# A two-round graph network kernel: 80 raw tiles per round instead of 64, the first 32 one per half iteration, and the raw bias added in place in PSUM

## The reference, cut to what matters

```python
h = relu(bn(x, gamma, beta))                 # batch norm over all nodes
h = einsum('nd,od->no', h, w) + b            # w is (T*D, D): 640 outputs per node
msg = h.reshape(N, T, D)[src, etype]         # one 128-wide row per edge
x = segment_sum(msg, dst, N)
```

## Time and profile before

| what | value |
|---|---|
| median of 3 runs | 6475.83 us |
| profiled execution | 6482.43 us |
| its span | 6480.6 us, mean granted TensorE clock 0.727 of 2.4 GHz |
| first round's gathers start | 164.42 us |
| raw gathers of round 2 start | 2074.29 us |
| second round's gathers start | 2181.80 us |

### The profile page before, as it was taken

One profiled execution on the slowest core, in us unless ns is written; L12 is line 12 of the kernel. 1 busy time (PEld: TensorE's weight loads), 2 busy tenths in 40 slices (PEclk: granted clock), 3 DMA queues, 4 the chain that ended last, 5 costly groups with the idle time before them and its releaser, 6 DMA issues. The chain is left out here.

```text
span 6480.6 us, 66649 instructions
## 1 busy us (share of the span) xinstructions
PE 4158.0 (64%) x17271; PEld 2806.2 (43%) x17271; DVE 3822.2 (59%) x7438; ACT 1611.9 (25%) x3872; POOL 4619.0 (71%) x4787
## 2 busy tenths in 40 slices
PE   7445454544445645455454555778777889999898
PEld 4333343433334434334343444333323346666696
DVE  6544444443334777776676666544444457777698
ACT  4000000000001200000000000576666656666504
POOL 5777777777777677777777777577777777777604
PEclk9555555555556755655555676898898889999999
DMA  9211121212223521221222333333333356777696
GB/s 342 53 52 52 52 53 52 52 52 55 65 65 117 188 52 52 53 52 52 52 52 53 86 90 92 99 117 110 110 110 110 110 174 217 220 219 216 208 315 211
DMA packets 432604, 726.45 MB, mean 112 GB/s; under 512 B 104654, under 2 KB 206576, under 8 KB 431506
## 3 DMA queue, kind: packets, MB, share of 16 engines
q1 hardware_dynamic: 281652, 400.74, 19.7%
q0 software_dynamic: 150592, 321.58, 17.0%
HBM read 509.16 MB, written 212.75 MB: 111 GB/s over the span
## 5 line engine op out<-in xcount | busy, mean ns | idle before, releaser
L573 POOL DMA_INDIRECT edge_rows<-messages,idx_stage x1504 | 1446.1, 961 | 487.1 <-issue 457.9
L1658 PE MATMUL banks<-onehot,edge_rows 128*128 128x128 f32 x3008 | 715.9, 413 | 995.7 <-DMA edge_rows<-messages,idx_stage 960.8
L1658 PEld LDWEIGHTS banks<-onehot,edge_rows 128*128 128x128 f32 x3008 | 613.8, 303 | 1117.2 <-DMA edge_rows<-messages,idx_stage 1082.0
L630 POOL DMA_INDIRECT sorted_rows<-edge_rows,idx_stage x784 | 760.3, 970 | 276.3 <-issue 238.2
L630 POOL DMA_INDIRECT sorted_rows<-buf_a,idx_stage x784 | 760.5, 970 | 260.5 <-issue 241.4
L573 POOL DMA_INDIRECT buf_x<-messages,idx_stage x747 | 717.4, 960 | 227.7 <-issue 227.7
L573 POOL DMA_INDIRECT buf_a<-messages,idx_stage x747 | 714.5, 957 | 227.7 <-issue 227.7
L1040 DVE TENSOR_TENSOR buf_a<-buf_a,banks 128x128 f32 x375 | 108.1, 288 | 1044.3 <-PE banks L1658 1005.4
L689 ACT ACTIVATE h_stage<-banks,bn_shift,bn_scale 128x128 f32<-128x128 f32 x128 | 58.6, 458 | 2521.1 <-PE banks L1599 2521.1
L1658 PE MATMUL banks<-x_onehot,buf_x 128*128 128x128 f32 x1494 | 355.9, 413 | 490.6 <-DMA buf_x<-messages,idx_stage 490.5
L1658 PE MATMUL banks<-x_onehot,buf_a 128*128 128x128 f32 x1494 | 344.8, 403 | 459.9 <-DMA buf_a<-messages,idx_stage 459.5
(11 more groups left out here) (201 smaller groups left out, 7088.3 us busy)
## 6 DMA issues: line engine op xcount, KB each, us to landing
buf_a<-sorted_rows SPq DMA_DIRECT2D x593, 288.0 KB, 4.0
messages<-work SPq DMA_DIRECT2D x196, 320.0 KB
buf_a<-dst_rows SPq DMA_DIRECT2D x198, 256.0 KB
buf_a<-in_attr SPq DMA_DIRECT2D x198, 128.0 KB, 2.5
buf_a<-h_in SPq DMA_DIRECT2D x396, 64.0 KB
edge_rows<-messages,idx_stage POOLq DMA_INDIRECT x1504, 2.5
sorted_rows<-edge_rows,idx_stage POOLq DMA_INDIRECT x784
sorted_rows<-buf_a,idx_stage POOLq DMA_INDIRECT x784
```

The lines of the kernel that those rows point to most:

```text
L573: nc.gpsimd.indirect_dma_start(gathered[p][h][:, t, :], None, source, bass.IndirectOffsetOnAxis(ap=idx_stage[:, h, t:t + 1], axis=0),).the ...
L630: nc.gpsimd.indirect_dma_start(sorted_rows, bass.IndirectOffsetOnAxis(ap=idx_stage[:, 2 * u + h, t:t + 1], axis=0), msg_halves[2 * u + h][ ...
L1658: last = nc.tensor.matmul(ps_sums[p][slot][j], rows_in_slot[:, j * GROUP_TILES + t, :], hot[:, j * GROUP_TILES + t, :], start=(t == 0), st ...
```

## The change

The number of raw tiles per round goes from 64 to 80 (`RAW_ITERS` from 4 to 5). The first 32 of them (`RAW_TWICE`) are processed one per half, the others one per two halves. Turn and transform of a tile now lie in the same half on TensorE, the turn before the second group and the transform behind it; bias, product and type sum are in VectorE's next half. The bias sum writes back into PSUM, the product reads it there, and `turn_raw` waits for the product. The masks and the types move to other free places, in two parts. The memsets of the accumulators are cut in two; in round 1 the first part runs ahead of the raw gathers, in round 2 likewise, after a wait for raw sums of round 1. The conv buffers `f_sb` and `msg_halves` move in `buf_a`; the row of ones in `f_sb` is written after round 2 instead of before it, and the first attribute loads follow the first `y` chunk. The slot of a half is now its number modulo 4, the first half of a round being half 10.

```diff
-RAW_ITERS = (4, 4)
+RAW_ITERS = (5, 5)
+RAW_TWICE = 2 * 16
-MSG_COLS = 16 * 512
+MSG_COLS = 20 * 512
...
+        def raw_tile(p, k):
+            n = k - 2 * RAW_ITERS[p]
+            if n >= RAW_TWICE:
+                n = RAW_TWICE + (n - RAW_TWICE) // 2 if n % 2 == 0 else -1
+            return n if 0 <= n < RAW_ITERS[p] * ITER_TILES else None
+        def raw_half(p, k):
+            t = raw_tile(p, k)
+            return t // HALF_TILES if t is not None and t % HALF_TILES == HALF_TILES - 1 else None
...
             load_x(0)
+            sp.wait_ge(s_y, 1)
+            load_x(1)
             for h in range(2):
                 load_attributes(h, h)
-            sp.wait_ge(s_y, 1)
-            load_x(1)
...
+            nc.gpsimd.memset(buf_a[:, 0:6 * WIDE], 0.0).then_inc(s_clear[0], 1)
             pool.wait_ge(s_edges_in, 64)
             pool.wait_ge(s_node_out, 16 * CHUNKS)
             gather_raw(0)
-            nc.gpsimd.memset(buf_a[:, :], 0.0).then_inc(s_clear[0], 1)
+            nc.gpsimd.memset(buf_a[:, 6 * WIDE:NBUF], 0.0).then_inc(s_clear[0], 1)
             for rnd in range(2):
                 if rnd == 1:
+                    pool.wait_ge(s_raw_agg, 2 * RAW_ITERS[0])
+                    pool.wait_ge(s_acc[0], SUMS + 2)
+                    nc.gpsimd.memset(buf_x[:, 0:RAW_TILES * P], 0.0).then_inc(s_clear[1], 1)
                     pool.wait_ge(s_node_out, 16 * CHUNKS * 2)
                     gather_raw(1)
                     pool.wait_ge(s_closed, 2)
-                    nc.gpsimd.memset(buf_x[:, :], 0.0).then_inc(s_clear[1], 1)
+                    nc.gpsimd.memset(buf_x[:, RAW_TILES * P:NBUF], 0.0).then_inc(s_clear[1], 1)
...
                 for t in range(T):
-                    link(nc.vector.tensor_scalar(raw_mask[:, :, t], raw_type, float(t), None, ALU.is_equal))
+                    for masks, types in zip(raw_masks, (raw_type[:, 0:masks_apart], raw_type[:, masks_apart:RAW_TILES])):
+                        link(nc.vector.tensor_scalar(masks[:, :, t], types, float(t), None, ALU.is_equal))
...
+        raw_biased = ps_raw.rearrange("p (t d) -> p t d", t=T)
...
-                nc.vector.tensor_tensor(raw_biased, ps_raw.rearrange("p (t d) -> p t d", t=T),
+                nc.vector.tensor_tensor(raw_biased, raw_biased,
                                         b_types[p][:, :].rearrange("p (t d) -> p t d", t=T), ALU.add).then_inc(s_raw_biased, 1)
...
-                nc.vector.tensor_tensor(raw_picked, raw_biased, raw_mask[:, t, :].unsqueeze(2).broadcast_to([P, T, D]),
+                mask = raw_masks[t >= masks_apart][:, t % masks_apart, :]
+                nc.vector.tensor_tensor(raw_picked, raw_biased, mask.unsqueeze(2).broadcast_to([P, T, D]),
...  round_half
+                t = None if beyond else raw_tile(p, k - 1)
-                    t = r - RAW_ITERS[p] - 1
-                    if h == 0 and 0 <= t < raw:
+                    if t is not None:
                         bias_raw(p, t)
...
-                    if h == 0 and 0 <= t < raw:
+                    if t is not None:
                         pick_raw(p, t)
...
-                    if h == 0 and 0 <= t < raw:
+                    if t is not None:
                         message_raw(p, t)
...  after the second round
+            nc.vector.memset(f_sb[RBF:RBF + 1, :, :, :], 1.0).then_inc(s_cut, 1)
...  turn_raw
-                    pe.wait_ge(s_raw_biased, n)
+                    pe.wait_ge(s_raw_picked, n)
...  aggregate
-                    if j and not beyond and 0 <= r - RAW_ITERS[p] < raw:
-                        (turn_raw, transform_raw)[h](p, r - RAW_ITERS[p])
+                    if j and raw is not None:
+                        turn_raw(p, raw)
...
+                    if raw is not None:
+                        transform_raw(p, raw)
```

More of the change, by code:

```diff
@@ L94 @@
 assert ITERS % 2 == 0 and FIRST_ITERS % 2 == 0 and CHUNK_ITERS % 2 == 0
-assert all(n % 2 == 0 and (2 * HALF_TILES // 2 + 1) * n + HALF_TILES + 2 <= CHUNK_ITERS + RAW_TILES for n in RAW_ITERS)
+assert all(2 * n + 2 * n * ITER_TILES - RAW_TWICE + 4 <= 2 * CHUNK_ITERS for n in RAW_ITERS)
 assert X_COLS * X_PARTS == N and X_COLS % BN_CHUNK == 0 and GROUPS % 4 == 0
@@ L215, in gnn_program @@
         x_in, squares, centred = (work[:, i * WIDE:(i + 1) * WIDE] for i in range(3))
-        square_sum, sd, rstd = (buf_a[:, 10432 + 8 * i:10436 + 8 * i] for i in range(3))
+        square_sum, sd, rstd = (buf_a[:, NPAD + 8 * i:NPAD + 4 + 8 * i] for i in range(3))
         h_rows = buf_a[:, 8 * WIDE:9 * WIDE]
@@ L566, in gather_pass @@
                     pool.wait_ge(s, v)
[L567 to L576, removed]
+                for half in range(2 * RAW_ITERS[p], 2 * ITERS):
+                    h = half % GATHER_SLOTS
+                    pool.wait_ge(s_idx[p], half + (1 - 2 * RAW_ITERS[p]))
+                    for t in range(LAST_TILES if half == 2 * ITERS - 1 else HALF_TILES):
+                        nc.gpsimd.indirect_dma_start(
+                            gathered[p][h][:, t, :], None, source,
+                            bass.IndirectOffsetOnAxis(ap=idx_stage[:, h, t:t + 1], axis=0),
+                        ).then_inc(s_gather[h][t // GROUP_TILES], 16)
             def gather_raw(p):
@@ L1225, in round_loop @@
                 whole = end // 2 - (end == ITERS)
-                for r2 in turns(dve, first // 2, whole, beyond):
+                for r in range(first, first + first % 2):
+                    bases = load_bases(r)
+                    for h in range(2):
+                        round_half(p, acc, r, r % 2, h, i, bases, beyond)
+                for r2 in turns(dve, (first + 1) // 2, whole, beyond):
                     for u in range(2):
@@ L1237, in hots_ahead @@
             def hots_ahead(p):
-                for half in range(1, AHEAD):
-                    build_onehot(p, 2 * RAW_ITERS[p] + half, half)
+                for half in range(2 * RAW_ITERS[p], 2 * RAW_ITERS[p] + AHEAD):
+                    build_onehot(p, half, half % GATHER_SLOTS)
             def count_beyond():
+                build_onehot(0, 2 * RAW_ITERS[0], 0)
                 raw_beyond(0, buf_a)
@@ L1637, in aggregate @@
                 r = r2 * 2 + u
-                turn, raw = r2 - RAW_ITERS[p] // 2, RAW_ITERS[p] * ITER_TILES
+                raw = None if beyond else raw_tile(p, r * 2 + h)
                 closing = isinstance(r2, int) and r2 == PAIRS - 1 and 2 * u + h == GATHER_SLOTS - 1
@@ L1663, in aggregate @@
                 else:
[L1664 to L1666 removed]
+                    if raw is not None:
+                        transform_raw(p, raw)
+                    if raw_half(p, r * 2 + h - 2) is not None:
+                        sum_raw(p, raw_half(p, r * 2 + h - 2))
             def mean(m):
@@ L1687, in round_loop @@
                 whole = end // 2 - (end == ITERS)
-                for r2 in turns(pe, first // 2, whole, beyond):
+                for r in range(first, first + first % 2):
+                    for h in range(2):
+                        aggregate(p, r // 2, r % 2, h, beyond)
+                for r2 in turns(pe, (first + 1) // 2, whole, beyond):
                     for u in range(2):
```

52 lines of the change are left out of this document (25 added, 27 removed).

## The result

The changed kernel takes 6464.02 us (median of 22 runs, 6458.64 to 6467.6) against 6474.41 for the kernel before beside it (22 runs, 6468.95 to 6478.03): ratio 0.9984, 95% interval 0.9977 to 0.9990, 10.4 us less. The forecast was +1.6.

What follows compares the result with a forecast made beforehand. POOL's gathers bound the rounds. -20.3 + 4.9 + 1.5 - 20.2 + 35.1 + 0.6 = +1.6 us, 6477.4 against the median 6475.83; range 6463 to 6491, with the faster cases 6440 to 6491.

Steps and rivals of the forecast that it cites:

- 32 gathers leave, -40.5: Both rounds on POOL: 16 gathers leave each, 20.3 and 20.2 us, 40.5 us less if the rest holds.
- Round 1's head: Before round 1's first gather: 16 more raw gathers start the round 4.9 us late; memset stretched beside VectorE's set-up, +1.5.
- Round 2's head: Before round 2's first gather: the early memset of 8.6 us fits 12.1 us of POOL idle, free, 3.5 to spare.
- The ring: Round 2, first 32 tiles: VectorE and PE wait on each other, period 11.17 us against POOL's 10.1; POOL loses 35.1 us.
- In-place sum and product: VectorE, bias sum and mask product with a PSUM operand in place of SBUF: same 0.82 us each, so nothing.
- Tail +0.6, conv 0: After round 2: moved 1.76 us memset before `scale_rows` adds 0.6 us; convolution buffers only change address, between -1 and +1.
- no ring (6442): Rival, chance 0.15: POOL's lead is larger or the product in time, no ring waits; -33.5 us, 6442.
- that PSUM in place costs: Rival, chance 0.14: same-bank read and write is dearer, 3.1 us per 0.1 us per tile; at 0.5 us, 6493.
- The ring at the upper clock (6445): Rival, chance 0.14: PE bursts raise its clock to 2.4 GHz, groups take 1.16 us, period 10.15, POOL loses 3; 6445.
- the likeliest case: The forecast itself, chance 0.57: ring at the slow clock, 6477.4 us, no change from before, own range 6463 to 6491.

Runs made afterwards that it cites:

- e15: Changed kernel with only the mask product moved ahead of the ranking in VectorE's half: 6433.34 us, ratio 0.9937 to the kernel before.
- e16: Changed kernel with only 4096 columns of round 2's memset ahead of the raw gathers, after the first h block is ready: 6457.22 us (0.9976).
- e14: Changed kernel with the bias sum written to SBUF again and the turn waiting for the bias alone: 6494.26 us (1.0032).
- e10: Changed kernel with the product ahead of the ranking and the early 10240-column memset as ten of 1024: 7861.30 us (1.0011), among TensorE's halts.
- e13: Kernel before (64 raw tiles) with the bias sum in place in PSUM, product reading it there, turn waiting for the product: 6461.07 us (0.9984).

## Why the forecast was wrong, step by step

The sum was +1.6 us, measured -10.4. The profiles differ by 19.0, of which 3 ns x 2966 gathers = 8.9 belong to the two executions; 10.1 are left, which agrees with the medians.

- *32 gathers leave, -40.5.* Right: in e15, without the ring, round 2 takes 1868.2 us for its 1483 gathers, 1.260 each.
- *Round 1's head, +4.9 and +1.5 for a stretched memset.* +4.9 measured, so the stretch was 0. The memset took 8.23 us, exactly its share, and VectorE paid: the index copy beside it took 6.83, and POOL waited 0.84 for it. Who is held was guessed the wrong way round. The 4.9 itself is in part chance: the raw gathers began 0.5 us earlier than before, and the wait for the copy took that back.
- *Round 2's head, "free, 3.5 us to spare".* Wrong by 6.2, some 5 by the held copy (e16 gives them back) and some 1 by the clock. The idle time was POOL's; it was filled by an instruction that held VectorE, on which that same idle time depended.
- *The ring, +35.1.* The mechanism is right in each part: spacing, idle time, clock, place, the releaser. The size is off by 10.6, the largest error of the sum: the period is 10.84, not 11.17 (1.99 in place of 2.20 from accumulate to bias, 2.45 in place of 2.56 for TensorE's part; 0.33 x 31 = 10.2; the 31 turns with their extras took 359.2 us and not 370.4), and the waits came to 24.5.
- *In-place sum and product, 0.* This is the step whose mechanism failed. I priced the two instructions by their own length, which indeed did not change (0.83, 0.82), and not by what they do to POOL, which bounds the round. It is worth 8.6 us against the kernel before (9.3 to 0.7), and at one tile per half it is worth 57 (e14 against e15): without it the 80 tiles would have made the kernel 20 us slower.
- *Not in the sum.* With other VectorE work beside them the gathers grew by 5.3 us, as the extra of all gathers fell only by 3.3 (16.9 to 13.7). It is round 1's counting: it lengthened 29 gathers by 3.7 us in all before and 79 by 9.7 after, less 1.0 that the round's slow first gather lost; in round 2 the rest went from 3.2 to 3.5.
- *Tail +0.6, conv 0.* +0.7 and -2.0.

Put together: -40.5 + 4.9 + 6.6 + 24.5 + 5.3 - 8.6 + 0.7 - 2.0 = -9.1, and -10.4 measured; the rest is within the interval. 6.6 is the head's 6.2 and 0.4 from the first raw gather to the first gather. The errors of the sum were -10.6 (ring), -8.6 (product), -1.5 (stretch) and -1.9 (tail and conv) on one side, +6.6 and +5.3 on the other. That the total missed by no more than 12 us is their cancelling, and luck.

Of the rivals, no ring (6442) is refuted by the waits, and that PSUM in place costs, by 0.82. The ring at the upper clock (6445) was half right: the burst does raise the clock, and the group in it takes 1.06, but TensorE's rest before the next turn brings back 0.50, and the group on which the ring hangs takes 1.93. The range held the time; the likeliest case had the ring's mechanism and missed a gain beside it.

The Trainium skill ("SBUF — State Buffer", the section "Who interferes with whom") says that VectorE and GpSimd have one pair of ports in common, that an instruction that needs it holds it for its whole length while the other engine stands, and that on VectorE's side these are copies in a two-port mode and, against a GpSimd instruction that reads SBUF, operations with two SBUF inputs. By that rule the trace agrees in three places: copy behind memset (8.00 for 0.16), gather behind product (1.48 for 0.95), and no hold where one operand is in PSUM (0.29, 0.57, 0.82). It does not show the rule in the other direction: a product that begins inside a gather is not held. I had applied the rule to the memset and not to the product.

## What to carry to other kernels

Where GpSimd bounds a stage, price each VectorE instruction by its operands too: one with two SBUF inputs, or a copy from SBUF to SBUF, delayed the gather that started inside it, and a GpSimd memset delayed such a copy until its end; with an operand in PSUM neither was seen. Where a wait closes a cycle through several engines, sum one turn from rows and compare it with the pace of the bound; then look for the link that can be moved forward in its engine's order, here two moved lines opened a ring that cost 24.5 us. An idle engine isn't free time if what it waits for runs on an engine that its new work holds.

## What the runs showed of the hardware

The phase rule of the gathers above (extra = product's end - gather's start - 0.12 us) gave prices from 0.07 to 0.35 us a product for one and the same pair of instructions, so a price from one schedule doesn't carry to another.

TensorE's halts came and went under one and the same program: the changed kernel took 6464.02 us without them and 7862.47 with them (e5, its timeline below). What causes them stays open.

```profile
2613.62 1.91 PE L1684 MATMUL banks<-onehot,edge_rows 128*128 128x128 f32 x8
...
2629.12 0.29 DVE L1062 TENSOR_TENSOR buf_x<-buf_x,banks 128x128 f32 x1 [30.54 <-remote]
...
2637.72 0.45 PE L1625 MATMUL banks<-ident,buf_a 128*128 128x128 f32 x1 [22.18 <-DVE work L1163]
```

Between 2600 and 3600 it stood 24 times for over 9 us, 299 us together; in the changed kernel's first trace never. Gathers and VectorE's instructions had their usual lengths. It was seen on four chips, and one of these (e10's) ran e13 to e16 without it. Order and size of differences between kernels were others there, so nothing was priced by those times.
